# The feed-forward bias b2 moves from a GpSimd addition into the second product on TensorE

## What is computed

```python
x1 = x + o.reshape(Bb, Tt, HEADS * DV) @ Wo            # attention with its residual
h2 = _ln(x1, ln_w, ln_b)
y  = x1 + gelu(h2 @ W1 + b1) @ W2 + b2                 # feed-forward; b2 has 128 numbers
x  = _layernorm(x + y)                                 # the sum that goes to the experts
...                                                    # gate, one expert per token, second layer norm
```

## Time and profile before

| | us |
|---|---|
| median of 3 runs | 496.59 (496.16 to 502.69) |
| span of the profiled execution, first to last instruction | 491.9 |
| median less span | 4.7 |
| PE busy | 418.2 (85%) |
| DVE busy | 365.8 (74%) |
| POOL busy | 346.4 (70%) |
| ACT busy | 345.9 (70%) |

### The profile page before, as it was taken

How to read it: one execution, slowest core, us unless ns; L and a number is a source line. 1 busy time by engine, 2 the same in 40 slices (tenths; PEclk the granted TensorE clock), 3 DMA queues, 4 the chain that set the end, 5 groups by cost and what they waited for, 6 DMA issues and landing times.

```text
span 491.9 us, 10725 instructions
## 1 busy us (share of the span) xinstructions
PE 418.2 (85%) x2755; PEld 339.0 (69%) x2755; DVE 365.8 (74%) x1205; ACT 345.9 (70%) x981; POOL 346.4 (70%) x393
## 2 busy tenths in 40 slices
PE   5868999999999988999999895002999999999994
PEld 3326776666666665778877685001999999999994
DVE  4378999998898989447778766820577787778884
ACT  2639688888889878878896876101577777777773
POOL 1146799999999989932366676744387788877785
PEclk9959999999999999999998985555899999999998
DMA  5566666655556443700011111272577777777730
GB/s 157 137 166 142 151 146 154 143 138 137 129 133 147 107 108 85 215 0 2 18 50 45 45 52 47 66 226 64 141 200 197 196 208 201 197 198 202 200 102 25
DMA packets 44669, 62.42 MB, mean 127 GB/s; under 512 B 6703, under 2 KB 30130, under 8 KB 42561
## 3 DMA queue, kind: packets, MB, share of 16 engines
q1 hardware_dynamic: 40000, 52.92, 42.4%
q0 software_dynamic: 4320, 8.47, 4.9%
q10 hardware_dynamic: 288, 0.34, 0.3%
HBM read 48.45 MB, written 13.71 MB: 126 GB/s over the span
## 4 chain that ended last, share of the span: by engine, by line
PE 43%; POOL 24%; issue 16%; DMA 7%; DVE 6%; ACT 3%; POOLq 0%; SPq 0%; ACTq 0%; DVEq 0%
PE bank L723 14%; PE bank L708 13%; POOL states L1690 12%; PE bank L379 5%; DMA expert_regions<-row_buffers,row_i 4%; POOL slab L1696 4%; POOL row_buffers L1681 3%; PE bank L355 3%; POOL x_sb L1708 3%; POOL expert_regions L573 2%; PE bank L714 2%; PE bank L986 1%; PE bank L392 1%; DMA kv<-values_by_head 1%; PE bank L1011 1%
## 5 line engine op out<-in xcount | busy, mean ns | idle before, releaser
L850 POOL DMA_INDIRECT out_rows<-x_sb x71 | 71.0, 999 | 35.8 <-issue 25.8
L573 POOL DMA_INDIRECT expert_regions<-row_buffers,row_i x64 | 63.2, 988 | 45.9 <-DMA expert_regions<-row_buffers,row_i 18.3
L723 PE MATMUL bank<-ew,x_sb 128*128 x568 | 79.9, 284 | 0.1
L1690 POOL TENSOR_TENSOR states<-states,queries 128x1024 f32<-128x1024 f32 x32 | 74.9, 2362 | 5.7 <-DVE states L1527 5.7
L708 PE MATMUL bank<-x_sb,slab 128*128 128x128 f32 x568 | 77.0, 280 | 0.9 <-ACT x_sb L737 0.9
L1527 DVE TENSOR_TENSOR_SCAN states<-bank,kv 128x512 f32<-128x512 f32 x64 | 73.0, 1203 | 0.1
L708 PEld LDWEIGHTS bank<-x_sb,slab 128*128 128x128 f32 x568 | 70.7, 196 | 1.6 <-issue 1.6
L723 PEld LDWEIGHTS bank<-ew,x_sb 128*128 128x128 f32 x568 | 69.4, 193 | 2.5 <-issue 0.3
L986 PE MATMUL bank<-states,con 128*128 128x256 f32 x256 | 60.4, 381 | 0.4 <-DVE row_buffers L1543 0.4
L804 DVE TENSOR_SCALAR x_sb<-bank,slab 128x128 f32<-128x128 f32 x142 | 42.8, 343 | 22.9 <-PE bank L708 22.9
L986 PEld LDWEIGHTS bank<-states,con 128*128 128x128 f32 x256 | 47.5, 190 | 7.7 <-issue 1.9
(11 more groups left out here) (188 smaller groups left out, 896.2 us busy)
## 6 DMA issues: line engine op xcount, KB each, us to landing
slab<-in_slabs SPq DMA_DIRECT2D x71, 258.0 KB, 3.1
kv<-values_by_head SPq DMA_DIRECT2D x32, 512.0 KB, 6.0
x_sb<-expert_regions SPq DMA_DIRECT2D x71, 65.0 KB, 2.9
x_sb<-in_x SPq DMA_DIRECT2D x32, 128.0 KB, 6.1
values_by_head<-row_buffers SPq DMA_DIRECT2D x16, 256.0 KB, 2.1
out_rows<-x_sb POOLq DMA_INDIRECT x71, 3.6
expert_regions<-row_buffers,row_i POOLq DMA_INDIRECT x64, 2.3
expert_regions<-pad_record SPq DMA_DIRECT2D x9, 65.0 KB, 3.4
```

Source lines behind the costliest of these rows:

```text
L573: pool.indirect_dma_start(out=regions, out_offset=bass.IndirectOffsetOnAxis(ap=row_i[:, q, g:g + 1].bitcast(U32), axis=0), in_=rec[:, ring ...
L723: ins = pe.matmul(bank[6 + s][:, 0:D], c_ht[:, s, c * P:(c + 1) * P], ew2[:, bass.ds(e * HC + c * D, D)], start=(c == 0), stop=(c == HC - 1))
L850: pool.indirect_dma_start(out=out, out_offset=bass.IndirectOffsetOnAxis(ap=c_id[:, q:q + 1].bitcast(U32), axis=0), in_=c_y[:, q, :], in_of ...
L1690: pool.tensor_tensor(half, half, queries[:, s, :].unsqueeze(1).to_broadcast([P, VL, T]), ALU.mult).then_inc(q_applied, 1)
```

## The change

b2 is split into three bfloat16 numbers whose sum gives it back (upper half of the float32, upper half of what is left, and again), one on each of partitions 0, 1 and 2 of `b2_rows`, copied four times along the free dimension. A matrix `three` has ones in rows 0 to 2 and zeros below. The product of the two, 128x128 by 128x512 in bfloat16, writes b2 for all 512 columns of bank 7 and opens the bank; the eight float32 products add to it. GpSimd's second addition and the semaphore between its two additions go. VectorE gets six memsets at the start of the program, and `split_b2` (two 128x128 operations and a copy to 128x512, each waiting for the one before) in step 7 of the attention loop.

```diff
+                    pe.wait_ge(b2_split.sem, 3)
                     pe.wait_ge(scanned, PAIRS)
+
+                pe.matmul(bank[7][:, :], three[:, :], b2_rows[:, :, :].rearrange("p g d -> p (g d)"), start=True, stop=False)
                 for g in range(4):
                     for m in range(2):
                         ins = pe.matmul(bank[7][:, g * P:(g + 1) * P], u_t[:, i % 2, m, g * P:(g + 1) * P], w2[:, m, :],
-                                        start=(m == 0), stop=(m == 1))
+                                        start=False, stop=(g == 3 and m == 1))
...
+            dve.memset(three[:, :], 0.0)
+            dve.memset(not_first[:, :], -1.0)
+            dve.memset(not_second[:, :], -1.0).then_inc(eps_ready, 1)
+            dve.wait_ge(eps_ready, 3)
+            dve.memset(three[0:3, :], 1.0)
+            dve.memset(not_first[0:1, :], 0.0)
+            dve.memset(not_second[0:2, :], 0.0).then_inc(eps_ready, 1)
...
+            def split_b2():
+                c = b2_split
+                c.start(0)
+                dve.wait_ge(late_ld, 16 * len(late_loads))
+                dve.wait_ge(eps_ready, 4)
+                c.link(dve.scalar_tensor_tensor(b2_left[:, :], b2[:, :].bitcast(BF16)[:, 1::2], not_first[:, :], b2[:, :],
+                                                ALU.mult, ALU.add))
+                c.join(dve)
+                c.link(dve.scalar_tensor_tensor(b2[:, :], b2_left[:, :].bitcast(BF16)[:, 1::2], not_second[:, :],
+                                                b2_left[:, :], ALU.mult, ALU.add))
+                c.join(dve)
+                c.link(dve.tensor_copy(b2_rows[:, :, :],
+                                       b2[:, :].bitcast(BF16)[:, 1::2].unsqueeze(1).to_broadcast([P, 4, D])))
+                c.end()
...
+                if k == 7:
+                    split_b2()
                 if on(5):
                     var_second(k - 5)
...
-                pool.tensor_tensor(xs, xs, xp[:, i % 2, :], ALU.add).then_inc(xp_added, 1)
-                if i == 0:
-                    pool.wait_ge(late_ld, 16 * len(late_loads))
-                pool.wait_ge(xp_added, i + 1)
-                pool.tensor_tensor(four(xs), four(xs), b2[:, :].unsqueeze(1).to_broadcast([P, 4, D]),
-                                   ALU.add).then_inc(x_summed, 1)
+                pool.tensor_tensor(xs, xs, xp[:, i % 2, :], ALU.add).then_inc(x_summed, 1)
```

More of the change, by code:

```diff
@@ L188, in gla_moe @@
         b1_raw, b1 = sb("b1_raw", [P, 2]), sb("b1", [P, 2])
-        b2 = sb("b2", [P, D])
+        b2, b2_left = sb("b2", [P, D]), sb("b2_left", [P, D])
+        b2_rows = sb("b2_rows", [P, 4, D], BF16)
+        three, not_first, not_second = sb("three", [P, P], BF16), sb("not_first", [P, 1]), sb("not_second", [P, 1])
         eps, one = sb("eps", [P, 1]), sb("one", [P, 1])
@@ L243, in gla_moe @@
             sem(n) for n in ("xp_ready", "ln2_stats", "ln2_var", "ln2_log", "ln2_rstd", "ln2_norm"))
-        t2_done, h2t_done, xp_added, x_summed = sem("t2_done"), sem("h2t_done"), sem("xp_added"), sem("x_summed")
+        t2_done, h2t_done, x_summed = sem("t2_done"), sem("h2t_done"), sem("x_summed")
         constants_ready = sem("constants_ready")
+        b2_split = Chain(sem("b2_split_chain"), 3)
         x_tok = a["x"].rearrange("(n b h p) d -> p n h b d", p=P, b=2, h=2)
```

## The result

The changed kernel takes 501.9 us (median of 13 runs, 495.3 to 505.1) beside 496.6 us for the kernel before on the same chip (13 runs, 494.5 to 502.7). The ratio is 1.010, with an interval of 1.007 to 1.013: the change costs about 5.0 us (3.5 to 6.5). Ratios leave out the executions of the chip's slower state, and so need not be those of the medians. I had forecast 498.7 us in a range of 496.0 to 502.3. The sign and the range held; of +2.15 us of forecast cost, the chip shows more than twice as much, and the excess lies in one step of the attention loop.

The account below looks back on a forecast made before the run. The prediction took the `o_rs` loop of 11.05 us, then TensorE until about 240 us, then the scatters as bounds. -0.2 + 0 + 0.6 + 1.5 + 0.25 = +2.15 us gave 498.7 us, range 496.0 to 502.3.

Parts of the forecast that it names:

- the likeliest case: Whole kernel: terms sum to +2.15 us, predicted time 498.7 us, own range 497.6 to 500, chance 55 in 100.
- rival C: Feed-forward scatters don't swallow late products, or TensorE's clock shifts: 2.3 to 3 us more, 501.0 to 501.7; 15 in 100.
- rival B: At 77.5 us `split_b2` waits for GpSimd's L1702 (short case, 500.0 us) or L1690 too (504.7); 13 in 100.
- the scatters as their own bound: From 240.9 to 335.0 us, 64 scatters 1.49 us apart form their own stream, hardly ever late for want of rows.
- The second addition costs nothing to remove: Attention loop, GpSimd: ten times the 1.27 us addition is covered by L1702's wait for `o_rs`, so removal gives 0 us.
- The -0.2 us at L1227: Behind the attention loop, ScalarE's L1227 no longer waits for GpSimd's L1696: -0.2 us, between -0.23 and 0.
- rival A: Attention loop: GpSimd's list, not `o_rs`, holds the step, so removing 1.27 us shortens it: 494 or nearer 491; 8 in 100.
- Six memsets: Program start, VectorE: covered by 1.33 us of idle time, taken as 0; 0.4 us if they cost 0.29 each.
- `split_b2` at +0.6 us: Attention step 7, VectorE: 1.2 us of operations, some 0.6 left after slack, delays the loop; +0.6 us, bounds 0 and 1.2.
- The bias product, 7 x 0.25 = 1.75 us: TensorE's second product: 0.25 us each; six ahead of the first scatter cost 1.5 us, the seventh, before batch 1, 0.25.
- the reading of the lead: Later batches: rows precede their scatters by 3.9 us, later 6.8, so the nine other bias products cost 0 at the end.
- The 4.7 us around the span: Whole kernel: 4.7 us between profiled span and median, added to the predicted span of 494.05 to give 498.7 us.

Follow-up runs that it names:

- e1: Kernel before without GpSimd's second addition, so b2 is added nowhere: 493.5 us beside 493.4, ratio 1.000.
- e11_split_step3: The changed kernel with `split_b2` still on VectorE but moved from step 7 to step 3: 495.9 us beside 495.4 for the kernel before, ratio 1.002.
- e4_pool_split: The changed kernel with `split_b2` on GpSimd, run once at 27.7 us: 495.3 us beside 493.4 for the kernel before, ratio 1.003.
- e9: Kernel before with three unused statistics operations in VectorE's step 7, where the change has its split: 495.6 us beside 494.7, ratio 1.002.
- e2: Kernel before with only the six memsets and `split_b2` in step 7, result unused, addition kept: 500.2 us beside 493.4, ratio 1.013.
- e10: Kernel before with ten unused statistics operations in VectorE's step 7: 499.6 us beside 494.7, ratio 1.008.
- e3: Kernel before with one bfloat16 product of zeros opening each of 16 banks, addition kept, no split: 494.5 us beside 493.4, ratio 1.001.
- e7: Kernel before with three products of zeros for each of pairs 0 to 5, addition kept, no split: 497.5 us beside 494.7, ratio 1.006.
- e6: Kernel before with three products of zeros for each of pairs 7 to 15, addition kept, no split: 494.0 us beside 494.7, ratio 0.999.
- e8: Kernel before with eight unused VectorE operations, each once beside GpSimd's pair L1690 and once with GpSimd idle; timed once, no kernel time given.

## Why the prediction was right, and where it was wrong

**The range held in part by luck.** The measured time is outside the likeliest case's own range of 497.6 to 500. It is inside the wide one because this was stretched to 502.3 for rival C, which cost nothing, and for rival B's short case of 500.0. What came is B's mechanism, with a cost of which B has only a part, and with a fall of the clock that the sum does not have. The two readings on which the forecast said it rested most, the scatters as their own bound and the price of the product, both held.

**The second addition costs nothing to remove: right.** It was argued from the wait for `o_rs` and the two loops of 11.05 us, and said that the idle time before L1702 would become about 18 us. It became 19.2 in the changed kernel and 18.6 with the addition's removal alone, and e1 measured 0. The -0.2 us at L1227 shows in the trace: the step that crosses 180 us takes 12.21 us in each of the five kernels without the addition there, 12.54 before. That 0.33 us is below what e1's interval resolves. The price of rival A, which is out, holds a slip: its 491.7 is the forecast less 7, so the rest of the change was in it already, and adding 2.35 again made 494; from 496.6 it would have been 492.

**Six memsets: right as far as seen.** `e11_split_step3` and `e4_pool_split`, which have them, cost 0.8 and 1.5 us by their ratios, products included, give or take 1.8 us; nothing separates the memsets from this.

**`split_b2` at +0.6 us: the step that failed.** The term was a sum of durations of operations alone: 1.2 us, less 0.6 of slack. The durations alone were right (1.11 us in e11 for my 1.2), and so was the slack (0.64 us in e9), though the rows gave only 0.43 of it, 0.32 and 0.11. What the likeliest case left out is that at 76.9 us GpSimd starts two operations in a row, and that VectorE's operations then last until those end. I had this as rival B, at 13 in 100, because no row showed it and the order at 77.5 was 0.05 us apart. The order was as close as that: L1734 started at 76.84, L1508 at 76.87. But I asked only what L1508 would wait for, the L1702 alone (500.0) or L1690 too (504.7). L1511 I had costed by L1543, whose inputs are not the same: L1543 reads a bank of PSUM and runs beside L1690 in each step at its usual speed, L1511 reads SBUF, and it waited for the first half of L1722. In the sum this is 3.05 us: 1.07 for L1508, the rest for L1511. The Trainium skill ("SBUF — State Buffer", Who interferes with whom) has an exclusive lock between VectorE and GpSimd that holds for whole instructions; by the probes, this case agrees (0.42 us became 1.96), and copies that read one tensor were held as well (0.42 became 1.87).

**A term that was missing: the clock, +1.6 us.** No part of the sum asked what TensorE does when L1573 is 4 us late. It idled 3.76 us and ran the next eight instructions at the lower level for most of their time: 3.61 instead of 1.99 us. Rival C spoke of the clock, but of the feed-forward stage. The step of `split_b2` is then 3.05 for the waits, plus 1.1 of its own work, less 0.64 of slack, plus 1.6 for the clock: 5.1 us, and the trace has 5.13. The clock's share is that of one execution: e2 lost 2.8 us by it in its profiled one, e10 2.7.

**The bias product, 7 x 0.25 = 1.75 us: right in place, a little high in price.** It takes 0.215 to 0.22 us from start to start, so six are 1.3 us; the traces have +1.1 from the first product on in the change and in e3, and +3.7 for eighteen in e7. That the nine later ones cost nothing was the reading of the lead; e6 with 27 of them measured -0.3 us (-1.7 to +1.1). The seventh is too small to be told from its neighbours. The Trainium skill's 216 ns ("TensorE: Matmul & The Clock Gate", Back-to-back issue gap) is what the trace shows; with it my seven would have been 1.5 us.

**The 4.7 us around the span: wrong, and by luck without harm.** I took the difference between the profiled span and the median of all runs. In the profiled executions of after, e1, e6, e8 and e10, 1.8 to 2.1 us lie around the span; the profiled execution of before was a quick one, of some 494 us. The predicted time stood on the median and is not moved by it, but a difference of two spans is not a difference of two medians: 7.9 against 5.3 here.

**The sum with measured terms**: -0.3 for the removal, 5.1 for `split_b2`, 1.3 for the products, 6.1 us, within the measured 3.5 to 6.5. On 496.6 us this makes 502.7.

## What to carry to other kernels

Before VectorE work is put into a full loop, look up what GpSimd runs at that minute: each VectorE operation tried here that read nothing but SBUF, copies too, lasted until the GpSimd `tensor_tensor` beside it had ended, so its price was that of its neighbour; only the statistics did not, nor do the operations of the loop that take one input from PSUM. A single late step can cost more than its delay: after an idle time of 3.76 to 4.17 us, and once of 1.90 us, TensorE came back at the lower level. And an engine's busy share does not tell what relief of it is worth: the wait just ahead of its next instruction in the loop does.

## What the runs showed of the hardware that I had not expected

- A VectorE operation with a single SBUF input also waits for GpSimd: bfloat16 copy 0.42 us alone and 1.87 beside L1690, `tensor_scalar` 0.28 and 1.82. The statistics don't (0.55 and 0.54).
- GpSimd lets the waiting operation in between two of its own; neither does VectorE wait for both, nor does GpSimd lose more than 0.2 us. So rival B's dearer case, a wait for the whole of L1690, isn't what happens to one operation.
- After TensorE had idled 3.76, 3.77 and 4.17 us (after, e2, e10), its next instructions ran at the lower level and cost 1.6, 2.8 and 2.7 us more; after 0.96 us (e9) none. In between, the length of the idle time just ahead does not decide: 1.90 us in e3 were followed by a slow spell, 1.92 us ahead of the output product at 174.56 us in e8 were not. In the tail, ahead of L952 (L958 after), 2.40 and 2.02 us were followed by one (after, e1), 2.42 us in e7 and 1.12 to 2.10 us in the ten other kernels were not. Whether the missing addition makes a dip there likelier (two of five kernels without it, none of eight with it), these runs don't settle.
- Open as well is why the first L1702 of the attention loop (L1734 after) starts at 42.5 us in some executions and at 43.7 in others of kernels that are the same up to there.
